# Low parts of transposed probabilities: one VectorE instruction over two PSUM banks in place of one for each bank

## The chip, the cores and the metric

The kernel runs on one core of one Trainium2 chip. The metric is the device time of one execution in microseconds; the median of three runs is given. A profile of one further execution shows each engine's instructions.

## The reference

A batch of 8 images of 128 channels and 32 x 32 positions (N = 1024) goes through two attention layers. All is float32.

```python
# layer 0
theta, phi, g = conv1x1(x, ...), conv1x1(x, ...), conv1x1(x, ...)   # each (B, 128, N)
attn = softmax(einsum('bcn,bcm->bnm', theta, phi), axis=-1)         # (B, N, N)
y = einsum('bnm,bcm->bnc', attn, g).reshape(B, 128, H, W)
z = (1 - w) * x + w * conv1x1(y, wz_w, wz_b)
# layer 1, on z
q, k, v = Wq @ z + bq, Wk @ z + bk, Wv @ z + bv                     # 16, 16 and 128 channels
att = softmax(einsum('bdi,bdj->bij', q, k) / sqrt(16), axis=-1)
out = gamma * einsum('bcj,bij->bci', v, att)
fused = Wf @ concat([out, z]) + bf
```

## The kernel before, in words

To keep float32's precision with the faster fp32r matmuls, an operand is split into a high part (rounded to fp32r) and a low part (the rest, full minus high), and a product is the sum of three matmuls: high x high, high x low, low x high.

**Units and blocks.** A unit is 128 query rows against all 1024 keys. Four units make a block: one layer, one image, one half of the queries. `BLOCKS` lists the 32 blocks, so there are 128 units. The blocks of the two layers alternate. Each engine runs the same hand-written order of steps: `emit(k)` for steps 0 to 19, a loop of 5 trips with 16 steps each, and the steps that are left. The engines meet only through semaphores.

**What happens to unit k.** TensorE makes its scores (two PSUM banks, `unit_scores`). VectorE takes the negated row maximum over both banks (`unit_max`, L751). ScalarE makes the exponentials into `probs` (`unit_exp`, L631). TensorE transposes `probs` in eight 128 x 128 pieces into `trans`, four for each of two PSUM banks (`unit_transposes`, L495). ScalarE copies each bank, rounded, to `pt_hi` (`unit_hi`, L640, two instructions). VectorE makes `pt_lo` = `trans` minus `pt_hi` (`unit_lo`, L761, two instructions, one for each bank). When a block's four units are through, `value_chunk` multiplies `pt_hi` and `pt_lo` by the values' two parts, in four chunks over the next steps (L519 to L521), into the PSUM bank `accum`.

**The order in a step.** On TensorE: scores of k; the small groups that the schedule puts before; the value chunks of the step; the small groups that it puts after; the transposes of k - 1. On ScalarE: the drain of `accum` where one is due; high parts of k - 2; exponentials of k - 1; the small groups. On VectorE: the drain of `accum` where one is due (L828, `o_sb`); a reciprocal once per block; the low parts of k - 2; the small groups before; the maximum of k; the small groups after. So on VectorE all that follows in a step is queued behind the low parts.

**What waits for the low parts.** The transposes of unit k overwrite `trans`, so before its bank 0 and again before its bank 1 TensorE waits for `pt_lo_ready` of unit k - 1 and that bank:

```python
for bank in range(2):
    if k >= 1:
        pe.wait_ge(pt_lo_ready, banks(k - 1, bank, it))
```

`value_chunk` waits for bank 1 of a block's last unit. The last block of all is different: its chunks are cut by bank and by pair of units, each waits for its own bank (`banks(TPB * gb + 2 * pair + 1, part, it)`), and nothing follows them but the last output.

**The small groups** are the projections and the like (theta, phi, g, y, z, qk, v, f, r). All use one PSUM bank, `misc`, one after the other, and TensorE begins one only when the one before has been drained (`misc_drained`). VectorE drains g (L788, L793), v (L793), y (L799), z (L807) and the second halves of qk (L773, L776), after which it copies a part of the keys (L779). GpSimd splits x, g, v, y and z in two parts; the z and y parts are matmul operands later. `r` turns the reciprocals into rows of `r_rows` by two matmuls (L566, L567), and `o_sb` (L828) is `accum` times `r_rows`; it sets `accum` free for the next block's first matmul.

Of the kernel before, what the change touches and what calls it, by code (L numbers as in the profile page):

```python
# [33 lines left out]
P = 128  # L34
HALF = N // 2
TPB = HALF // P
KT = N // P
CPB = 4
# [144 lines left out]
def build(nc, x, x_tiles, weights_t, columns, qk_bias, g_bias, gates, out):  # L183
    f32, f32r = mybir.dt.float32, mybir.dt.float32r
    ALU, ACT, AX = mybir.AluOpType, mybir.ActivationFunctionType, mybir.AxisListType

    with ExitStack() as ctx:
        def sb(name, shape, dt=f32):
            return ctx.enter_context(nc.sbuf_tensor(name, shape, dt))

        def sem(name):
            return ctx.enter_context(nc.semaphore(name))
# [41 lines left out]
        pt_hi = sb("pt_hi", [P, 2, KT, HALF], f32r)  # L234
        pt_lo = sb("pt_lo", [P, 2, KT, HALF], f32r)
# [44 lines left out]
        trans = ctx.enter_context(nc.psum_tensor("trans", [P, N], f32))  # L280
# [24 lines left out]
        pt_hi_ready = sem("pt_hi_ready")  # L305
        pt_lo_ready = sem("pt_lo_ready")
        pv_done = sem("pv_done")
# [29 lines left out]
        def banks(k, bank, it):  # L337
            return 2 * k + bank + 1 + 2 * PERIOD * it
# [4 lines left out]
        def chunks(gb, c, it):  # L343
            return CPB * gb + c + 1 + PERIOD * it
# [17 lines left out]
        def cols(h):  # L362
            return slice(h * HALF, (h + 1) * HALF)

        def f(ap):
            return ap.bitcast(f32)
# [344 lines left out]
        def _(dve):  # L711
# [41 lines left out]

            def unit_lo(k, it):
                gb, t = divmod(k, TPB)
                for bank in range(2):
                    dve.wait_ge(pt_hi_ready, banks(k, bank, it))
                    if t == 0 and bank == 0 and gb >= 2:
                        dve.wait_ge(pv_done, chunks(gb - 2, CPB - 1, it))
                    at = (slice(None), gb % 2, slice(4 * bank, 4 * bank + 4), slice(t * P, (t + 1) * P))  # L760
                    nc.vector.tensor_tensor(pt_lo[at], trans[:, cols(bank)].rearrange("p (n q) -> p n q", n=4),  # L761
                                            f(pt_hi[at]), ALU.subtract).then_inc(pt_lo_ready, 1)

            def small(group, it):
                kind, b, h = group
# [53 lines left out]
            def emit(k, it):  # L819
# [25 lines left out]
                if 0 <= k - 2 < UNITS:  # L845
                    unit_lo(k - 2, it)
# [155 lines left out]
```

## Time and profile before

| | |
|---|---|
| median of 3 runs | 548.36 us (548.23 to 548.5) |
| the profiled execution, its own time | 549.02 us |
| its span, first to last instruction | 547.2 us |
| TensorE busy | 521.3 us, 95% |
| its weight loads | 436.5 us, 80% |
| VectorE busy | 431.9 us, 79% |
| ScalarE busy | 373.1 us, 68% |
| GpSimd busy | 303.4 us, 55% |
| granted TensorE clock | 1.00 over the whole span |

In the profile PE is TensorE's matmuls, PEld its weight loads, DVE is VectorE, ACT ScalarE, POOL GpSimd. Matmuls overlap their neighbours in the trace, so a matmul's own duration is longer than its step in the stream. Consecutive VectorE or ScalarE instructions overlap a little too. L761 is line 761 of the kernel. Times in the timeline are microseconds from the start of the span; `xN` merges N consecutive alike instructions into one row, whose duration is from the first one's start to the last one's end.

### The profile page before, as it was taken

What the parts mean: (1) busy time and instruction counts of PE and PEld (TensorE: products, weight loads), DVE (VectorE), ACT (ScalarE), POOL (GpSimd) and SP (SyncE); (2) the same over time, 40 slices, a digit from 0 to 9 for tenths busy, and PEclk for the clock granted to TensorE, in tenths of its full rate; (3) what the DMA queues carried; (4) which work ended last, traced back from release to release, by engine and by line L of the source; (5) the groups of instructions that cost most, each with busy time, mean ns of one, the idle gap of its engine ahead of it and who ended that gap; (6) DMA issues with size and microseconds to landing.
All of it is one profiled execution on the core that took longest, in us unless ns stands there. A gap on an engine that the chain in (4) does not pass through costs nothing.

```text
span 547.2 us, 9717 instructions
## 1 busy us (share of the span) xinstructions
PE 521.3 (95%) x2933; PEld 436.5 (80%) x2933; DVE 431.9 (79%) x633; ACT 373.1 (68%) x668; POOL 303.4 (55%) x288
## 2 busy tenths in 40 slices
PE   7898899999999989999899998999999999899996
PEld 5677778887888878888788887888788888687886
DVE  5948687798777887888877888679887787989973
ACT  4765577568785678657777577765878557878773
POOL 1576257684277743875448752579426780274442
PEclk9999999999999999999999999999999999999999
DMA  5000000011000100002000020000200010000011
GB/s 171 26 36 2 0 1 0 2 41 59 0 22 0 62 34 0 19 0 96 0 0 19 0 96 0 0 19 4 91 0 0 19 40 20 0 2 20 1 40 38
DMA packets 5782, 13.41 MB, mean 25 GB/s; under 512 B 1024, under 2 KB 1536, under 8 KB 5760
## 3 DMA queue, kind: packets, MB, share of 16 engines
q1 hardware_dynamic: 5616, 13.00, 7.0%
q8 instruction: 12, 0.20, 0.2%
q10 hardware_dynamic: 144, 0.13, 0.1%
q14 instruction: 10, 0.08, 0.1%
HBM read 8.93 MB, written 4.19 MB: 24 GB/s over the span
## 4 chain that ended last, share of the span: by engine, by line
PE 82%; ACT 7%; DVE 5%; issue 4%; POOL 1%; DMA 1%; ACTq 0%; DVEq 0%
PE trans L495 18%; PE accum L519 10%; PE accum L521 9%; PE accum L520 9%; PE scores L485 5%; PE scores L460 5%; PE scores L462 4%; PE scores L461 4%; PE misc L460 3%; PE misc L546 3%; PE misc L462 3%; PE misc L461 3%; ACT probs L631 3%; ACT pt_hi L640 2%; DVE pt_lo L761 2%
## 5 line engine op out<-in xcount | busy, mean ns | idle before, releaser
L761 DVE TENSOR_TENSOR pt_lo<-trans,pt_hi 128x512 fp32r<-128x512 f32 x256 | 164.6, 685 | 56.3 <-ACT pt_hi L640 54.7
L640 ACT ACTIVATE pt_hi<-trans 128x512 fp32r<-128x512 f32 x256 | 139.7, 596 | 74.0 <-PE trans L495 72.8
L751 DVE TENSOR_REDUCE neg_max<-scores 128x1 f32<-128x1024 f32 x128 | 155.6, 1215 | 1.1 <-PE scores L462 1.1
L495 PE MATMUL trans<-ident,probs 128*128 128x128 f32 x1024 | 135.2, 274 | 13.3 <-DVE pt_lo L761 7.3
L631 ACT ACTIVATE probs<-scores,neg_max 128x1024 f32<-128x1024 f32 x128 | 143.7, 1123 | 4.9 <-DVE neg_max L751 4.5
L495 PEld LDWEIGHTS trans<-ident,probs 128*128 128x128 f32 x1024 | 115.3, 141 | 28.4 <-DVE pt_lo L761 9.9
L519 PE MATMUL accum<-pt_hi,g_hi 128*128 128x512 f32 x136 | 54.3, 400 | 0.0
L521 PE MATMUL accum<-pt_hi,g_lo 128*128 128x512 f32 x136 | 53.5, 394 | 0.0
L520 PE MATMUL accum<-pt_lo,g_hi 128*128 128x512 f32 x136 | 53.3, 392 | 0.0
L460 PE MATMUL scores<-phi_hi,theta_hi 128*128 128x512 f32 x112 | 49.0, 437 | 0.2 <-POOL phi_lo L879 0.2
L866 POOL TENSOR_TENSOR theta_hi<-proj_full,zero 128x512 fp32r<-128x512 f32 x14 | 14.6, 1041 | 57.7 <-ACT proj_full L659 57.7
L462 PE MATMUL scores<-phi_hi,theta_lo 128*128 128x512 f32 x112 | 44.2, 395 | 0.0
L461 PE MATMUL scores<-phi_lo,theta_hi 128*128 128x512 f32 x112 | 43.8, 391 | 0.0
L519 PE MATMUL accum<-pt_hi,v_hi 128*128 128x512 f32 x96 | 38.8, 404 | 0.0
L793 DVE TENSOR_TENSOR values_full<-misc,values_full 128x256 f32<-128x256 f32 x64 | 27.1, 423 | 14.0 <-ACT values_full L653 11.9
L521 PE MATMUL accum<-pt_hi,v_lo 128*128 128x512 f32 x96 | 37.7, 392 | 0.0
L520 PE MATMUL accum<-pt_lo,v_hi 128*128 128x512 f32 x96 | 37.6, 392 | 0.0
L866 POOL TENSOR_TENSOR y_hi<-y_full,zero 128x512 fp32r<-128x512 f32 x16 | 16.7, 1041 | 33.6 <-DVE y_full L799 33.6
L866 POOL TENSOR_TENSOR z_hi<-z_full,zero 128x512 fp32r<-128x512 f32 x16 | 16.7, 1041 | 32.9 <-DVE z_full L807 32.9
L485 PE MATMUL scores<-k_op,q_op 96*128 96x512 f32 x96 | 34.2, 437 | 0.0
L521 PEld LDWEIGHTS accum<-pt_hi,g_lo 128*128 128x128 f32 x136 | 25.5, 188 | 5.8
L519 PEld LDWEIGHTS accum<-pt_hi,g_hi 128*128 128x128 f32 x136 | 25.5, 188 | 5.4
(161 smaller groups left out, 1037.2 us busy)
## 6 DMA issues: line engine op xcount, KB each, us to landing
x_keep<-x_dram SPq DMA_DIRECT2D x8, 512.0 KB, 3.4
out_dram<-o_sb SPq DMA_DIRECT2D x15, 256.0 KB, 2.0
x_raw<-x_tiles_dram SPq DMA_DIRECT2D x7, 512.0 KB, 3.7
x_raw<-x_tiles_dram SPq DMA_DIRECT2D x2, 256.0 KB, 3.8
w_all<-weights_t_dram SPq DMA_DIRECT2D x1, 336.0 KB, 3.7
out_dram<-o_sb SPq DMA_DIRECT2D x2, 128.0 KB, 1.9
w_all<-weights_t_dram ACTq DMA_DIRECT2D x1, 128.0 KB, 3.9
g_bias_rows<-g_bias_dram SPq DMA_DIRECT2D x1, 64.0 KB, 3.4
```

The source lines that it names most:

```text
L460: nc.tensor.matmul(dst, hi_l, hi_r, start=True, stop=False)
L461: nc.tensor.matmul(dst, hi_l, lo_r, start=False, stop=False)
L462: return nc.tensor.matmul(dst, lo_l, hi_r, start=False, stop=True)
L485: last = nc.tensor.matmul(dst, q_of(b)[0:KROWS, q0:q0 + P], k_of(b)[0:KROWS, cols(half)], start=True, stop=True)
L495: last = nc.tensor.transpose(trans[:, n * P:(n + 1) * P], probs[:, k % 2, n * P:(n + 1) * P], ident[:, :])
L519: nc.tensor.matmul(dst, hi[:, tile], p_hi, start=(n == 0), stop=False)
L520: nc.tensor.matmul(dst, hi[:, tile], p_lo, start=False, stop=False)
L521: last = nc.tensor.matmul(dst, lo[:, tile], p_hi, start=False, stop=(n == KT - 1))
L631: nc.scalar.activation(probs[:, k % 2, :], scores[:, k % 2, :], ACT.Exp, bias=neg_max[:, k % 4:k % 4 + 1], accum_out=row_sum[:, slot(gb), ...
L640: nc.scalar.activation(pt_hi[:, gb % 2, 4 * bank:4 * bank + 4, t * P:(t + 1) * P], trans[:, cols(bank)].rearrange("p (n q) -> p n q", n=4) ...
L751: nc.vector.tensor_reduce(neg_max[:, k % 4:k % 4 + 1], scores[:, k % 2, :], AX.X, ALU.max, negate=True).then_inc(max_ready, 1)
L761: nc.vector.tensor_tensor(pt_lo[at], trans[:, cols(bank)].rearrange("p (n q) -> p n q", n=4), f(pt_hi[at]), ALU.subtract).then_inc(pt_lo_r ...
```

## The change

`unit_lo` no longer goes bank by bank. It waits until the high parts of both banks are there, and one instruction of 1024 columns subtracts them from both banks of `trans`. Its semaphore rises by 2, so that all who wait for a bank still count alike. The wait for the value chunks of two blocks earlier, which frees the buffer of `pt_lo`, stands before that one instruction as it stood before the first of two.

```diff
             def unit_lo(k, it):
                 gb, t = divmod(k, TPB)
-                for bank in range(2):
-                    dve.wait_ge(pt_hi_ready, banks(k, bank, it))
-                    if t == 0 and bank == 0 and gb >= 2:
-                        dve.wait_ge(pv_done, chunks(gb - 2, CPB - 1, it))
-                    at = (slice(None), gb % 2, slice(4 * bank, 4 * bank + 4), slice(t * P, (t + 1) * P))
-                    nc.vector.tensor_tensor(pt_lo[at], trans[:, cols(bank)].rearrange("p (n q) -> p n q", n=4),
-                                            f(pt_hi[at]), ALU.subtract).then_inc(pt_lo_ready, 1)
+                dve.wait_ge(pt_hi_ready, banks(k, 1, it))
+                if t == 0 and gb >= 2:
+                    dve.wait_ge(pv_done, chunks(gb - 2, CPB - 1, it))
+                at = (slice(None), gb % 2, slice(None), slice(t * P, (t + 1) * P))
+                nc.vector.tensor_tensor(pt_lo[at], trans[:, :].rearrange("p (n q) -> p n q", n=KT),
+                                        f(pt_hi[at]), ALU.subtract).then_inc(pt_lo_ready, 2)
```

## Rows read from the trace of the kernel before

**Rows 1.** The page: busy time by engine, and the chain's shares by engine.
```profile
PE 521.3 (95%) x2933; PEld 436.5 (80%) x2933; DVE 431.9 (79%) x633; ACT 373.1 (68%) x668; POOL 303.4 (55%) x288
...
PE 82%; ACT 7%; DVE 5%; issue 4%; POOL 1%; DMA 1%; ACTq 0%; DVEq 0%
```

**Rows 2.** The chain in order of time (start, duration, what), one unit's transposes.
```profile
252.56 0.88 PE trans L495 x8
```

**Rows 3.** The page's groups: busy us, mean ns | idle before, releaser.
```profile
L761 DVE TENSOR_TENSOR pt_lo<-trans,pt_hi 128x512 fp32r<-128x512 f32 x256 | 164.6, 685 | 56.3 <-ACT pt_hi L640 54.7
...
L751 DVE TENSOR_REDUCE neg_max<-scores 128x1 f32<-128x1024 f32 x128 | 155.6, 1215 | 1.1 <-PE scores L462 1.1
...
L793 DVE TENSOR_TENSOR values_full<-misc,values_full 128x256 f32<-128x256 f32 x64 | 27.1, 423 | 14.0 <-ACT values_full L653 11.9
```

**Rows 4.** The waits: who <- for whom, us in total, times, longest.
```profile
DVE pt_lo L761 <- ACT pt_hi L640: 54.7, 77, 3.4
...
PEld trans L495 <- DVE pt_lo L761: 9.9, 15, 1.6
...
PE trans L495 <- DVE pt_lo L761: 7.3, 6, 1.4
```

**Rows 5.** Timeline, a plain unit (start, duration, engine, line, what).
```profile
282.91 1.09 ACT L640 ACTIVATE pt_hi<-trans 128x512 fp32r<-128x512 f32 x2 [0.60 <-PE trans L495]
...
283.54 1.29 DVE L761 TENSOR_TENSOR pt_lo<-trans,pt_hi 128x512 fp32r<-128x512 f32 x2 [0.86 <-ACT pt_hi L640]
...
284.75 1.22 DVE L751 TENSOR_REDUCE neg_max<-scores 128x1 f32<-128x1024 f32 x1
...
285.72 1.03 PE L495 MATMUL trans<-ident,probs 128*128 128x128 f32 x8
```

**Rows 6.** Timeline, behind the key copy; one of five such places.
```profile
261.73 2.41 DVE L779 CAST k_op<-k_op 32x512 fp32r<-32x512 f32 x1
...
264.17 1.29 DVE L761 TENSOR_TENSOR pt_lo<-trans,pt_hi 128x512 fp32r<-128x512 f32 x2
264.92 0.42 PEld L495 LDWEIGHTS trans<-ident,probs 128*128 128x128 f32 x4 [1.59 <-DVE pt_lo L761]
...
265.51 0.42 PEld L495 LDWEIGHTS trans<-ident,probs 128*128 128x128 f32 x4 [0.18 <-DVE pt_lo L761]
```

**Rows 7.** Timeline, drains of z and of the accumulator in one loop trip.
```profile
315.10 0.75 DVE L807 SCALAR_TENSOR_TENSOR z_full<-misc,gate,x_keep 128x512 f32<-128x512 f32 x1
315.54 1.09 ACT L640 ACTIVATE pt_hi<-trans 128x512 fp32r<-128x512 f32 x2 [1.24 <-PE trans L495]
...
316.24 0.39 PE L566 MATMUL misc<-diag_hi,ones_r 128*128 128x512 f32 x1
...
318.50 0.68 DVE L828 TENSOR_TENSOR o_sb<-accum,r_rows 128x512 f32<-128x512 f32 x1
...
319.44 0.40 PE L519 MATMUL accum<-pt_hi,g_hi 128*128 128x512 f32 x1
```

**Rows 8.** Timeline near the start: what TensorE waited for.
```profile
21.05 0.38 PE L546 MATMUL misc<-w_parts,x_hi 128*128 128x256 f32 x1 [1.01 <-DVE values_full L793]
...
24.85 1.16 PE L495 MATMUL trans<-ident,probs 128*128 128x128 f32 x8 [0.55 <-DVE pt_lo L761]
```

**Rows 9.** Timeline in the last 85 us, a z drain and the matmul behind it.
```profile
478.54 0.74 DVE L807 SCALAR_TENSOR_TENSOR z_full<-misc,gate,x_keep 128x512 f32<-128x512 f32 x1
...
479.50 0.28 PE L546 MATMUL misc<-wv_parts,z_hi 128*128 128x256 f32 x1
```

**Rows 10.** Timeline, transposes released by the exponential with low parts close behind.
```profile
505.08 1.29 DVE L761 TENSOR_TENSOR pt_lo<-trans,pt_hi 128x512 fp32r<-128x512 f32 x2
...
506.14 0.86 PEld L495 LDWEIGHTS trans<-ident,probs 128*128 128x128 f32 x8 [1.07 <-ACT probs L631]
```

**Rows 11.** Timeline, the last unit and the last block's first matmul.
```profile
539.62 1.29 DVE L761 TENSOR_TENSOR pt_lo<-trans,pt_hi 128x512 fp32r<-128x512 f32 x2 [1.93 <-ACT pt_hi L640]
...
540.37 0.39 PE L519 MATMUL scores<-pt_hi,g_hi 128*128 128x256 f32 x1 [0.98 <-DVE pt_lo L761]
```

## The prediction

> **What bounds the kernel now.** I read the page's shares of busy time and its chain first. TensorE is busy for 95% of the span and holds 82% of the chain that ended last; VectorE is busy for 79% and holds 5% of it [rows 1]. So the end is set by TensorE's instruction stream plus the places where that stream stops. VectorE's length as such sets nothing: it is the question of when single VectorE instructions end. The chain prices TensorE's stream: the eight transposes of a unit take 0.88 us when nothing stops them, 0.11 each [rows 2].
>
> Then the groups: the low-part subtractions are 256 instructions of 685 ns, the row maxima 128 of 1215 ns over 1024 columns, and a subtraction-like TENSOR_TENSOR with 256 columns takes 423 ns [rows 3]. Then the waits: VectorE stood idle 54.7 us for the high parts that ScalarE makes, in 77 pieces; TensorE and its weight load stood idle 7.3 and 9.9 us for the low parts, in 6 and 15 pieces [rows 4]. VectorE has time to spare where it waits for ScalarE; TensorE's stops behind it are short and few.
>
> The timeline shows a plain unit [rows 5]. ScalarE makes the two banks' high parts back to back from 282.91, 1.09 us for both. VectorE starts on bank 0 at 283.54, right after the first of them, and runs bank 1 behind it until 284.83; the two halves of the work are a pipeline over the two engines. Only at 285.72 does TensorE come to the next transposes, which overwrite the banks: 0.89 us of slack. The row maximum is queued behind the low parts on VectorE and starts when they end.
>
> **The change part by part.** One instruction of 1024 columns replaces two of 512. Its own duration is not in the trace. From 256 to 512 columns the time grows by 262 ns, so 1024 columns make 685 + 524 = 1209 ns; the maximum over 1024 columns of the same PSUM banks takes 1215 [rows 3]. I take 1.21 us. The pair takes 1.29 us from first start to last end [rows 5], because the second starts under the tail of the first. Bounds: 1.37 us, twice 685, from above; from below 1.07, which is 1024 columns at the 1.02 ns that each further column costs, with almost no fixed part left (1.05).
>
> Removed: 0.08 us of VectorE per unit, 10 us over 128 units, of a 79% busy engine. Where VectorE waits for ScalarE this is worth nothing. Added: the instruction waits for the second bank's high parts. In the plain unit these end at 284.00; a start 0.03 later, as the first low part shows, gives 284.03 to 285.24, against 284.83 [rows 5]. So bank 1's low part ends 0.42 us later, bank 0's about 1.0 later, and the maximum with everything queued behind it on VectorE starts 0.42 later until VectorE next waits for something else. In the plain unit nothing needs this: the transposes have 0.89 us in hand. That covers most units, as the few stops in [rows 4] say.
>
> The move of the wait on the values two blocks earlier costs nothing: that block ended four units before. The signal rises by two in place of one twice; the counts on TensorE's side are the same, but its wait for bank 0 is now met only with bank 1's. No DMA is moved.
>
> The Trainium skill ("Perfetto Trace Analysis", section Optimizing Scalar/DVE Operations) says that larger operations help where the engine is saturated, and that breaking up instructions may let work complete sooner where Vector is not saturated but causes bubbles on other engines. The trace agrees with the second half as the case here (79% busy, stops of TensorE behind the low parts); by the first half alone the change would gain the 1.3 us of rival 3 below.
>
> Where it is on the path, in order of weight:
>
> (a) Once per trip of the loop, five times, the copy of the keys takes 2.41 us, with GpSimd splitting x at its side. The low parts behind it start at 264.17 and end 265.46; TensorE has been idle for 1.59 us and starts four transposes at 264.92, the other four at 265.51, 0.05 after the second low part [rows 6]. After: one instruction 264.17 to 265.38, the first four at 265.43, the second four after 4 x 0.11 = 0.44 at 265.87. That is 0.36 later. VectorE is saturated here and the 0.08 is gained, but it is outweighed since half of the transposes no longer run under the second low part. 5 x 0.36 = 1.8.
>
> (b) Also once per trip, VectorE drains a misc group and the accumulator just in time. z_full ends 315.85, TensorE needs it at 316.24; with 0.42 more and the 0.05 signal it starts at 316.32, a stop of 0.08. The high parts of the next unit end at 316.63, so again VectorE is 0.42 late; o_sb then ends at 319.18 + 0.42 = 319.60, and the first matmul of the next block moves from 319.44 to 319.65 [rows 7]. Together 0.22 per trip, 1.1 for five, and 0.1 for still smaller margins of 0.02 to 0.05 us elsewhere in the trips.
>
> (c) The start. VectorE is full from the first unit's low parts on (setup work). Its 0.42 reaches the drain for which TensorE waited 1.01 us before 21.05, and the next transposes, which waited for the low parts like the 24.85 ones [rows 8], lose (a)'s 0.36: 0.78 together, which I take as 0.75. One more place like (a) in this stretch has a free 0.36. The y drain near 66 us, queued behind the low parts and read by GpSimd before TensorE can go on, loses 0.23; two small ones 0.15. Sum 1.5.
>
> (d) The last 85 us. The z drain that ends at 479.28 releases a matmul at 479.50: with 0.42 and 0.05 it is 479.75, a stop of 0.25 [rows 9]; three drains of this kind I take at 0.25, 0.2 and 0.05 (the first of them again z, the others o_sb). Five transposes wait for the exponential with the low parts close behind: low parts 505.08 to 506.37, transposes at 506.14. After, 506.29 plus 0.05 is 506.34, 0.2 later for the first four and 0.15 for the last four [rows 10]; 0.7 for five. And the last unit: the last block's value matmuls begin on bank 0 alone at 540.37, 0.06 after the first low part's end at 540.31 [rows 11]. With the high parts' second half 0.49 later and 1.21 us for the whole it is 541.32 plus 0.06: 1.0 us later, and nothing after it hides that. Sum 0.25 + 0.5 + 0.7 + 1.0 = 2.45.
>
> Total 1.8 + 1.2 + 1.5 + 2.45 = 6.95, say 7.0 us. The profiled execution took 549.02 us with a span of 547.2; its own time plus 7.0 is 556.0. The runs' median is 548.36, 0.66 below the profiled one, so I state 555.4.
>
> At 1.07 us instead of 1.21 each of (a) to (d) shrinks by 0.14 where it exists: about 5 x (0.22 + 0.08) at the trips, 0.9 at the start, 1.6 at the end, 4.0 in all. At 1.37 each grows by 0.16, and transposes that have only 0.10 to 0.18 in hand after the change begin to stop too: about 1.3 per trip, 2.0 at the start, 3.5 at the end, 12.0 in all.
>
> **Rivals.**
>
> 1. Only the direct losses stay (transposes and value matmuls that waited for the low parts), and the drains are absorbed, for instance because matmul ends are modelled and TensorE's true need is later than shown. Then 1.8 at the trips, 1.1 at the start, 0.7 + 1.0 at the end: 4.6 us, 553.0. For it: the margins in (b) are of 0.1 to 0.2 us. Against it: the drains stand behind an in-order queue, and TensorE's stream around them has no gap.
>
> 2. The instruction costs as much as the two did (1.37), or its effects feed on each other through ScalarE: 12 us, 560.4. Against it: the 1215 ns maximum over the same banks [rows 3].
>
> 3. It gets faster. The mechanism: fewer instructions, 0.08 us saved in each unit in which VectorE is the bound. At the bound of all 128 units this would be 10 us, but the chain gives VectorE 5% [rows 1], and only about 16 units have low parts that queue behind other VectorE work: 16 x 0.08 = 1.3 us, 547.1. It decides from the point at which TensorE gets nothing from the early release of bank 0. In [rows 6] it does start on it, 0.59 us before the rest, and the last block does as well [rows 11]; I see no place where only VectorE's sum counts. The Trainium skill ("VectorE: DVE Perf Modes", section Rules for kernel authors) advises to minimize the op count; by that rule it would come out this way.
>
> 4. No difference: all 0.42 us delays find slack and (a) is made good by the saved 0.08 and by later gaps. 548.4. Against it stands the last unit's 1.0 us, which no gap follows.
>
> **How the numbers follow.** My forecast 0.57 (its own range 554 to 557.5), rival 1 0.20, rival 2 0.14, rival 3 0.04, no difference 0.05. What a measurement of this kernel can tell from no change is about 0.2%, 1.1 us. Faster 0.04, same 0.05, slower 0.91. The range takes in rival 1 and the 1.07 bound (552.4) below, and goes most of the way to rival 2 above: 551.8 to 559.5.
>
> **What would show it.** 128 low-part instructions of about 1.21 us; VectorE's busy time down, its idle time for the high parts up by well over 20 us. In the five places behind the key copy, transposes that start as one run of eight, with TensorE's idle time before them about 0.5 us longer. New stops of TensorE at the `r` group, at the first matmul of a block behind o_sb, and at v groups behind z_full. The last block's first matmul, 0.75 us after the last pair of low parts began, would come 1.27 us after the one instruction's start. A duration near 1.37, or low parts that start later than 0.05 us after the high parts, would make the prediction too low; TensorE idle for low parts unchanged would make it too high.

## The result and the profile after

The changed kernel takes 565.08 us, median of 4 runs (562.94 to 569.53), against 548.43 (548.23 to 549.88) for the kernel before: ratio 1.0305, 95% interval 1.027 to 1.0339, so 3% slower. The direction was forecast; the time lies outside the stated range of 551.8 to 559.5 and the rise is 16.7 us where 7.0 was forecast. The profiled execution took 562.94 us with a span of 561.1, 13.9 more than the span of before.

The page of the changed kernel, busy time and chain:

```profile
PE 527.9 (94%) x2933; PEld 438.1 (78%) x2933; DVE 420.8 (75%) x505; ACT 372.6 (66%) x668; POOL 303.4 (54%) x288
...
PE 78%; DVE 8%; ACT 6%; issue 5%; POOL 1%; DMA 1%; ACTq 0%; DVEq 0%
```

Against [rows 1] VectorE is busy 11 us less with 128 instructions fewer, and yet its share of the chain rises from 5 to 8%. TensorE is busy 6.6 us more for the same 2933 matmuls. Nobody gave it work: some of its matmuls ran slower. That was the first sign of what the prediction had no term for.

The groups and the waits of the changed kernel, which answer to [rows 3, 4]:

```profile
L760 DVE TENSOR_TENSOR pt_lo<-trans,pt_hi 128x1024 fp32r<-128x1024 f32 x128 | 156.8, 1225 | 100.6 <-ACT pt_hi L640 90.7
```

```profile
DVE pt_lo L760 <- ACT pt_hi L640: 90.7, 97, 3.6
...
PE trans L495 <- DVE pt_lo L760: 19.3, 20, 2.0
...
PEld trans L495 <- DVE pt_lo L760: 13.0, 15, 2.2
```

The merged instruction takes 1225 ns; 1.21 us had been taken for it. What VectorE saved it spent waiting for ScalarE: 36 us more of idle time in front of the low parts. TensorE waits for the low parts 19.3 us in 20 places, where it was 7.3 in 6, and the longest such stop grew from 1.4 to 2.0 us.

A plain unit after the change, for [rows 5]:

```profile
290.99 1.09 ACT L640 ACTIVATE pt_hi<-trans 128x512 fp32r<-128x512 f32 x2 [0.60 <-PE trans L495]
292.18 1.23 DVE L760 TENSOR_TENSOR pt_lo<-trans,pt_hi 128x1024 fp32r<-128x1024 f32 x1 [0.93 <-ACT pt_hi L640]
293.32 1.21 DVE L751 TENSOR_REDUCE neg_max<-scores 128x1 f32<-128x1024 f32 x1
293.80 1.03 PE L495 MATMUL trans<-ident,probs 128*128 128x128 f32 x8
```

The high parts end at 292.08 and the low parts start at 292.18, 0.10 later; the trace of before had led me to expect 0.03. From the first high part's start to the low parts' end it is 2.42 us, where it was 1.92: VectorE's queue is 0.50 us late in each such unit, not 0.42. The transposes still come in time here, with 0.39 us in hand.

Behind the key copy, for [rows 6], once at TensorE's full clock and once, one trip earlier, as it also happened:

```profile
201.19 2.36 DVE L778 CAST k_op<-k_op 32x512 fp32r<-32x512 f32 x1
...
203.57 1.23 DVE L760 TENSOR_TENSOR pt_lo<-trans,pt_hi 128x1024 fp32r<-128x1024 f32 x1
204.85 1.57 PEld L495 LDWEIGHTS trans<-ident,probs 128*128 128x128 f32 x8 [2.20 <-DVE pt_lo L760]
204.85 1.97 PE L495 MATMUL trans<-ident,probs 128*128 128x128 f32 x8 [2.05 <-DVE pt_lo L760]
...
206.47 0.78 PE L460 MATMUL scores<-phi_hi,theta_hi 128*128 128x512 f32 x1
...
271.86 1.23 DVE L760 TENSOR_TENSOR pt_lo<-trans,pt_hi 128x1024 fp32r<-128x1024 f32 x1
273.13 0.86 PEld L495 LDWEIGHTS trans<-ident,probs 128*128 128x128 f32 x8 [2.14 <-DVE pt_lo L760]
```

In both places the eight transposes now start as one run after the low parts' end. In this document a stop is the idle time of TensorE's matmuls, here the 2.05 us in the row of PE at 204.85; its weight load stood idle 2.20. At 273.13 their weight loads take 0.86 us, at 204.85 they take 1.57, and the next scores matmul 0.78. The windows of the changed kernel around the earlier place (columns as in their first line) say why:

```profile
core 0: us, PE busy (x) PEld busy (x) DVE busy (x) ACT busy (x) POOL busy (x), PEclk, DMA share, GB/s
200.00:204.00 4.00, 2.81 (x15) 2.25 (x13) 3.90 (x4) 3.58 (x7) 3.19 (x2) 1.00 0.00 0
204.00:208.00 4.00, 3.15 (x12) 2.86 (x13) 2.79 (x5) 2.17 (x4) 1.34 (x3) 0.59 0.00 0
208.00:212.00 4.00, 4.00 (x23) 3.41 (x22) 2.31 (x3) 1.55 (x4) 1.11 (x2) 0.98 0.00 0
```

After a stop of 2.05 us TensorE's granted clock is 0.59 in the next 4 us, that is the lower level of 1.2 GHz most of the time, and the unit and its successor together come 1.6 us later than the same two do at the other four trips. Before the change the same stops were of 1.2 to 1.4 us and the granted clock stayed at 1.00.

The drains, for [rows 7]:

```profile
323.89 0.74 DVE L806 SCALAR_TENSOR_TENSOR z_full<-misc,gate,x_keep 128x512 f32<-128x512 f32 x1
324.75 0.19 PEld L566 LDWEIGHTS misc<-diag_hi,ones_r 128*128 128x128 f32 x1 [0.48 <-issue]
324.76 0.49 PE L566 MATMUL misc<-diag_hi,ones_r 128*128 128x512 f32 x1
...
327.30 0.68 DVE L827 TENSOR_TENSOR o_sb<-accum,r_rows 128x512 f32<-128x512 f32 x1
...
328.03 0.19 PEld L519 LDWEIGHTS accum<-pt_hi,g_hi 128*128 128x128 f32 x1 [0.26 <-DVE o_sb L827]
```

Both stops that (b) named are there. Their price was set too low: the drain's signal reaches the weight load 0.12 us after z_full's end (0.05 after o_sb's), and the weight load now starts only behind the stop. The matmul takes 0.49 us where it took 0.39 [rows 7], and the next one follows it after 0.33 us instead of 0.23. The g drain ahead of z's matmuls had shown the longer way of the signal before the change: it ends at 301.47 and the weight load follows 0.13 later.

```profile
301.05 0.42 DVE L793 TENSOR_TENSOR values_full<-misc,values_full 128x256 f32<-128x256 f32 x1
...
301.60 0.19 PEld L460 LDWEIGHTS misc<-y_hi,w_parts 128*128 128x128 f32 x1
```

Close behind the exponential, for [rows 10], and the last unit, for [rows 11]:

```profile
516.90 1.22 DVE L760 TENSOR_TENSOR pt_lo<-trans,pt_hi 128x1024 fp32r<-128x1024 f32 x1
518.24 0.86 PEld L495 LDWEIGHTS trans<-ident,probs 128*128 128x128 f32 x8 [1.35 <-ACT probs L631]
518.27 0.95 PE L495 MATMUL trans<-ident,probs 128*128 128x128 f32 x7 [0.95 <-DVE pt_lo L760]
...
553.01 1.22 DVE L760 TENSOR_TENSOR pt_lo<-trans,pt_hi 128x1024 fp32r<-128x1024 f32 x1 [2.38 <-ACT pt_hi L640]
554.28 0.19 PEld L519 LDWEIGHTS scores<-pt_hi,g_hi 128*128 128x128 f32 x1 [2.30 <-DVE pt_lo L760]
```

Near 518 the low parts end at 518.12 and the transposes follow 0.12 later: they, and no longer the exponential alone, release them. At the last unit the first matmul comes 1.27 us after the low parts' start, as forecast.

Laying the two traces over each other, unit by unit at the last of its eight transposes, gives where the 13.9 us of the profiled execution came from. Worked out from the starts of those transposes:

```
stretch                                   after - before   forecast
ahead of the first low part                    1.7            -
start, up to the first loop trip               1.5           1.5
five loop trips, without the next line         5.1           3.0
lower clock after the stop at 204.85           1.6            -
behind the loop, with the last unit's 1.1      3.9           2.45
```

The first 1.7 us lie ahead of the first low part, where both programs are the same. TensorE's matmuls follow each other there at 0.43 us in place of 0.23 for some microseconds longer. First the kernel before, then the changed one:

```profile
7.60 0.40 PE L460 MATMUL scores<-x_hi,w_parts 128*128 128x512 f32 x1
...
7.83 0.40 PE L461 MATMUL scores<-x_lo,w_parts 128*128 128x512 f32 x1
```

```profile
7.36 0.63 PE L460 MATMUL scores<-x_hi,w_parts 128*128 128x512 f32 x1
...
7.79 0.63 PE L461 MATMUL scores<-x_lo,w_parts 128*128 128x512 f32 x1
```

0.63 us and a step of 0.43 are also what such a matmul takes at the lower clock behind the stop at 204.85 (207.05, 207.47), so this too is TensorE at its lower level. The profile prints 1.00 there because the traces hold no record of the clock before 5.05 us (before) and 10.17 us (after), and the steps are of 0.43 us ahead of these places and of 0.23 behind them; "1.00 over the whole span" in the table of before is to be read so. This long start is no effect of the change. Of the fourteen traces of this case ten start so, with the first transposes at 16.0 to 16.5 us, and in six of these nothing is merged; the other four have them at 14.3 to 14.5, and one of the four is merged from the first unit on. Nor is the kernel before free of the clock's fall later on: 12 of the 56 executions of it that were run beside the experiments have a granted clock of 0.997, as the profiled one of the changed kernel has with its one fall. Of these 12 there is no trace.

### The profile page after: what moved, and what is told of

The parts are those of the page before. It is cut to its first block, busy times and chain, and to the rows that moved or that the text cites. A ratio compares the mean times of both kernels' runs of the same rounds, so it can differ in the third digit from the quotient of the medians.

```text
span 561.1 us, 9612 instructions
## 1 busy us (share of the span) xinstructions
PE 527.9 (94%) x2933; PEld 438.1 (78%) x2933; DVE 420.8 (75%) x505; ACT 372.6 (66%) x668; POOL 303.4 (54%) x288
## 2 busy tenths in 40 slices
DMA packets 5782, 13.41 MB, mean 24 GB/s; under 512 B 1024, under 2 KB 1536, under 8 KB 5760
## 4 chain that ended last, share of the span: by engine, by line
PE 78%; DVE 8%; ACT 6%; issue 5%; POOL 1%; DMA 1%; ACTq 0%; DVEq 0%
PE trans L495 17%; PE accum L519 9%; PE accum L521 9%; PE accum L520 9%; PE scores L460 5%; PE scores L462 4%; PE scores L461 4%; PE scores L485 4%; DVE pt_lo L760 4%; PE misc L460 3%; PE misc L546 3%; PE misc L462 3%; PE misc L461 3%; ACT pt_hi L640 3%; PE misc L547 1%
## 5 line engine op out<-in xcount | busy, mean ns | idle before, releaser
L760 DVE TENSOR_TENSOR pt_lo<-trans,pt_hi 128x1024 fp32r<-128x1024 f32 x128 | 156.8, 1225 | 100.6 <-ACT pt_hi L640 90.7
L495 PE MATMUL trans<-ident,probs 128*128 128x128 f32 x1024 | 135.0, 275 | 19.3 <-DVE pt_lo L760 19.3
L865 POOL TENSOR_TENSOR z_hi<-z_full,zero 128x512 fp32r<-128x512 f32 x16 | 16.7, 1041 | 37.6 <-DVE z_full L806 37.5
L865 POOL TENSOR_TENSOR y_hi<-y_full,zero 128x512 fp32r<-128x512 f32 x16 | 16.7, 1043 | 34.8 <-DVE y_full L798 34.8
L865 POOL TENSOR_TENSOR g_hi<-values_full,zero 128x512 fp32r<-128x512 f32 x18 | 18.8, 1044 | 20.9 <-DVE values_full L792 20.9
```

Of the source, the lines that this page charges most:

```text
L495: last = nc.tensor.transpose(trans[:, n * P:(n + 1) * P], probs[:, k % 2, n * P:(n + 1) * P], ident[:, :])
L760: nc.vector.tensor_tensor(pt_lo[at], trans[:, :].rearrange("p (n q) -> p n q", n=KT), f(pt_hi[at]), ALU.subtract).then_inc(pt_lo_ready, 2)
L865: return nc.gpsimd.tensor_tensor(hi, full, zero[:, :].broadcast_to([P, full.shape[1]]), ALU.add)
```

## The experiments

Each ratio is to runs of the kernel before on the same chip, given with its median.

**Both halves wait for both high parts.** Two instructions stay, but start when the merged one would.

```diff
-                    dve.wait_ge(pt_hi_ready, banks(k, bank, it))
+                    dve.wait_ge(pt_hi_ready, banks(k, 1, it))
```

> Two low-part instructions as before the change, but both wait for the high parts of both banks. Theory (timing): the loss comes from when VectorE starts and from TensorE being released late, not from the merged instruction. Then this kernel, whose second low part ends even some 0.07 us later than the merged one, must be slower than before by 6 to 8 us (555 to 557), with the stops behind the key copy unchanged at about 1.4 us (there the high parts are long ready) and a granted clock of 1.00. Rival (size): one instruction over two PSUM banks is itself what costs. Then this is within 1 us of before, 548.4.

555.69 us against 549.60, ratio 1.0098 (1.0065 to 1.0131), granted clock 1.00 in three executions and 0.997 in two, where 1.00 had been expected. The longest stop of TensorE for low parts is 1.5 us. Nothing is merged here and most of the direct loss in the loop's drains is there: the same transposes as in the changed kernel come 0.20, 0.30 and 0.1 us late in each trip, those behind the key copy are within 0.16 us of where they were. The rival (the large instruction as such) falls.

**Both halves at their times, TensorE told only at the end.**

```diff
-                                            f(pt_hi[at]), ALU.subtract).then_inc(pt_lo_ready, 1)
+                                            f(pt_hi[at]), ALU.subtract)
+                    if bank == 1:
+                        last.then_inc(pt_lo_ready, 2)
```

> Two low-part instructions at their old times, but TensorE is told of both only when the second has ended. Theory (timing): this isolates the loss of bank 0's early release. VectorE's queue is untouched. Key copy: 5 x 0.4 = 2.0 us; three such places in the first 80 us 1.1; five transposes close behind the exponential 0.7; last block 0.6. Sum 4.4, so 552.8; the stop behind the key copy becomes 2.0 us, and if such a stop is what lowers TensorE's clock, 0 to 5 us more and a granted clock below 1.00 in some executions. Rival (size): 548.4, no change.

557.22 us, ratio 1.0128 (1.0088 to 1.0168), granted clock 0.990 to 0.993 in all four executions. The trace against that of before: 0.5 us at two units near the start, 0.3 to 0.45 behind the key copy, 0.34 at three of the five units close behind the exponential, nothing at the drains; about 4 us in all up to the last unit. Another 3.1 us lie at the low clock after two stops of 1.93 us, of which this is the first:

```profile
267.57 1.29 DVE L761 TENSOR_TENSOR pt_lo<-trans,pt_hi 128x512 fp32r<-128x512 f32 x2
268.92 1.25 PEld L495 LDWEIGHTS trans<-ident,probs 128*128 128x128 f32 x7 [2.08 <-DVE pt_lo L761]
```

The two parts add up, nearly: without start and clock the trace of both_wait is 5.1 us late at the last unit's transposes and that of late_signal 4.0; the changed kernel's is 9.5.

**The changed kernel with two halves behind the key copy.** `unit_lo` takes the old form for k == 26, which in the loop is that unit of each trip.

> The changed kernel, but with two instructions in the one unit per loop trip whose low parts stand behind the key copy. Theory (timing and clock): the stop there stays at about 1.4 us, each trip gives back 0.4 to 0.5, and TensorE's clock stays at 1.00: 557 to 559, with runs close together. Rival (clock by chance): the clock still falls to 0.98 to 0.99 in some executions and the runs spread over several us as those of the changed kernel did (562.9 to 569.5).

560.08 us, ratio 1.0196 (1.0152 to 1.024), 5.0 us below the changed kernel's median. That is above the 557 to 559 expected. In the trace the stops there are again 1.2 to 1.4 us and the clock does not fall behind them; the runs spread over 2.4 us where the changed kernel's spread over 6.6. The clock was not at 1.00, though (0.996 to 0.997 in all four): in the trace it fell once behind another stop, of 1.83 us near 474 us, at which the exponential of ScalarE is late as well. The kernel before has that stop too, of 1.80 us, and its trace passed it at full clock.

**A longer stop and nothing merged.**

```diff
+                if k == 26:
+                    nc.vector.tensor_tensor(scratch[:, :], w_all[:, 0:HALF], w_all[:, 256:256 + HALF], ALU.add)
                 for bank in range(2):
```

> The kernel before, nothing merged, with one more VectorE instruction (a sum of two pieces of the weights into a scratch tile that nobody reads, about 0.7 us) ahead of the low parts behind the key copy, once per loop trip. TensorE's stop there grows from 1.4 to about 2.1 us: 5 x 0.65 = 3.2 us, 551.7 by length alone. Theory (clock by length of the stop): the granted clock falls below 1.00 in some executions and the runs spread, up to 5 us more. Rival (clock by chance, or only by the merged instruction): 551.7 and 1.00 in all.

560.40 us, ratio 1.0179 (1.0136 to 1.0221), granted clock 0.985 to 0.988 in all four. In the trace four of the five lengthened stops (1.91 to 2.11 us; the fifth is 1.84) are followed by the lower clock, and so is the stop of 1.82 us near 480 us, at about 1.6 us each. The second one:

```profile
202.54 0.69 DVE L758 TENSOR_TENSOR scratch<-w_all 128x512 f32<-128x512 f32 x1
203.24 1.29 DVE L764 TENSOR_TENSOR pt_lo<-trans,pt_hi 128x512 fp32r<-128x512 f32 x2
203.99 0.42 PEld L496 LDWEIGHTS trans<-ident,probs 128*128 128x128 f32 x4 [2.26 <-DVE pt_lo L764]
```

Its windows have the granted clock at 1.00, then 0.59:

```profile
200.00:204.00 4.00, 1.89 (x12) 1.48 (x10) 3.92 (x5) 3.08 (x5) 2.23 (x1) 1.00 0.00 0
204.00:208.00 4.00, 4.00 (x15) 3.24 (x16) 3.25 (x6) 2.29 (x4) 1.61 (x4) 0.59 0.00 0
```

So 0.7 us of VectorE work in five places costs about 10 us (by the ratio 9.8, 7.5 to 12.1), where some 8 at most had been expected: in the trace five lowered clocks came on top of the longer stops. The clock falls because TensorE stood still for long, not because of the merged instruction.

**The merged instruction in the unit behind the key copy alone.** k == 26 only.

> The kernel before, with the merged instruction only in the unit behind the key copy, five units in all. Theory (gate and clock): about 0.45 us directly in each, 2.2 us, and stops of 1.9 us that lower the clock in several of them at 1.0 to 1.6 us each: 551 to 556, clock 0.99. Theory without the clock: 550.6 and 1.00.

556.13 us, ratio 1.0119 (1.0077 to 1.016), granted clock 0.987 to 0.997, three lowered clocks in the trace, behind stops of 1.90, 1.90 and 1.81 us. The time is at the upper end of what was expected, 551 to 556. Five instructions of 128 carry a good third of the change's whole loss.

**The merged instruction where it is covered.** 28 <= k < 33, 25 units.

> The kernel before, with the merged instruction only in five units per loop trip (25 of 128) at whose transposes the changed kernel's trace shows no shift. Theory (a VectorE that waits gives nothing back): within 0.2% of before, clock 1.00. Rival (each merged unit saves or costs by itself): 2 us less (25 x 0.08) or about 2.7 us more (25/128 of the whole loss).

549.02 us against 550.18, ratio 0.9998 (0.9978 to 1.0018). In the trace the last unit's transposes are 0.03 us from where they were. The 2 us that VectorE saves are worth nothing, and a delay of 0.5 us costs nothing either where TensorE comes later anyway.

**The merged instruction in the last unit alone.** k == 127.

> The kernel before, with the merged instruction only in the last of the 128 units, in front of the last block's value matmuls, which start on bank 0's low part. Theory: the last block's first matmul 1.0 to 1.1 us later and the end with it, as nothing follows that could hide it: 549.5 on runs of 548.4, the stop there 2.1 us in place of 1.0. Rival (the end is set by r_rows or the store): no change.

Ratio 1.0023 (1.0008 to 1.0037), that is 1.3 us with an interval of 0.4 to 2.0; TensorE's stop ahead of the last block is 2.07 us.

**The changed kernel again.**

> The changed kernel once more, on the same chip as the run beside it, to see the spread of its clock. Theory: the direct loss of some 10.6 us is in every execution, on top come 0 to 2 us at the start as in the kernel before, and 1 to 1.6 us for each stop of about 2 us after which the clock is lowered, one to five of them: 561 to 569, with the granted clock between 0.98 and 1.00 and the longer times at the lower clocks. Rival (the spread is not the clock): times and granted clocks unrelated.

564.82 us, ratio 1.0295 (1.0239 to 1.0351). Over the eight executions of the changed kernel, time and granted clock go together:

```
us      562.82  562.94  562.98  564.04  566.12  566.67  569.53  569.84
clock   0.997   0.997   0.994   0.990   0.990   0.990   0.981   0.984
```

The profiled one has three lowered clocks inside the loop, behind stops of 1.92, 2.03 and 2.10 us, and stands 3.7 us behind the other at the last unit.

**Taking the stop away.** The key copy is slow only beside GpSimd's split of x. First the split was moved two steps later.

```diff
-SPLIT_X = {3: 1, 14: 2, **{LOOP_FROM + PERIOD * (i - 2) + 9: i + 1 for i in range(2, B - 1)}}
+SPLIT_X = {3: 1, 14: 2, **{LOOP_FROM + PERIOD * (i - 2) + 11: i + 1 for i in range(2, B - 1)}}
```

> The kernel before, nothing merged, with GpSimd's split of the next x two steps later in the loop, after its work on the reciprocals, so that it no longer runs beside VectorE's key copy. The copy should take about 0.42 us in place of 2.4, the low parts behind it start some 2 us earlier, and TensorE's stop of 1.4 us per trip go. The next projections need the split only some 2 us after its new end. Theory (the key copy's stop is the place where a low part decides): 5 x 1.1 to 1.4 = 5.5 to 7 us less than before, 541.5 to 543. Rival (GpSimd or ScalarE is late next): 546 to 549.

546.93 us against 550.18, ratio 0.9944 (0.9928 to 0.9959). The first copy now takes 0.42 us and 1.7 us come back in each trip, but the second key copy of the trip has become the slow one:

```profile
270.82 2.40 POOL L873 TENSOR_TENSOR x_lo<-x_raw,x_hi 128x1024 fp32r<-128x1024 f32 x1
...
271.31 2.18 DVE L779 CAST k_op<-k_op 32x512 fp32r<-32x512 f32 x1
...
274.27 0.42 PEld L495 LDWEIGHTS trans<-ident,probs 128*128 128x128 f32 x4 [1.19 <-DVE pt_lo L761]
```

It gives 1.05 back, so that neither my estimate nor its rival held: the collision moved. The Trainium skill ("SBUF — State Buffer", section SBUF: two separate sides) says that VectorE and GpSimd share a port pair that one of them holds alone; by the 0.42 us without and 2.0 to 2.4 us with a neighbour, the traces agree, and the slow copy above ends 0.27 us after GpSimd's instruction does (273.49 and 273.22).

The same later split under the changed kernel:

> The changed kernel (merged instruction) with the same later split of x. Theory: the direct loss and the lowered clock behind the key copy go with the stop, the losses at the drains stay: 541.5 to 543 plus some 8 to 9 us (0.6 per trip, 1.5 at the start, 3.9 at the end), so 550 to 552, the clock lowered at most once near 468 us (a stop of 2.0 us there). Rival (the merged instruction spoils the clock wherever it stands): 556 or more and a clock of 0.99.

558.37 us, ratio 1.0169 (1.0137 to 1.0202), granted clock 0.997 to 1.000. By the medians that is 11.4 us above late_split, but the median of late_split lies between two groups of its executions (545.65 to 546.33 and 547.54 to 548.17). Both traces have the long start, and their spans of 556.6 and 546.4 are 10.3 us apart: the direct loss by itself, at the full clock. I had expected 550 to 552. The later split gave less than I thought, and behind the two key copies the merged instruction still loses some 0.4 us per trip.

Then the split was held until the first copy is done, and so lies between the two.

```diff
                 pool.wait_ge(x_loaded, 16 * b + 16 * it)
+                if b >= 3:
+                    pool.wait_ge(k_copied, halves(b - 2, 0, it))
```

In guarded_split the wait stood ahead of the loop too (b == 2, for both copies); guarded_loop has it as shown.

> The kernel before, nothing merged; GpSimd's split of the next x keeps its place but waits for the key copy beside which it ran (k_copied), so that it lies between the two key copies of a trip. The later split only moved the collision to the second copy (2.18 us there, TensorE 1.05 us later per trip). Theory: both copies take 0.42 us, no such stop is left: 1.6 us less per trip than before, 8 us, and about 0.5 us less in the first 80 us: 540 to 542, clock 1.00. Rival (the reciprocals' split on GpSimd, now 1 to 2 us later, is late for the r group): 543 to 547.

> As guarded_split, but with the wait for the key copy only in the loop. Ahead of the loop the wait had put the split 4 us later and the next step 1.8 us back, against 0.3 gained. Theory: another 1.5 us less, 541.5 to 542.5. Rival (the lost 1.8 us is made good later anyway): 543.4.

guarded_split: 543.39 us, ratio 0.9886 (0.9867 to 0.9906), where 540 to 542 had been expected; 1.8 us were lost ahead of the loop. guarded_loop: 542.33 us against 550.04, ratio 0.9857 (0.9834 to 0.988), granted clock 1.00 in all five. Its trace at a key copy:

```profile
260.20 0.42 DVE L779 CAST k_op<-k_op 32x512 fp32r<-32x512 f32 x1
...
260.65 1.29 DVE L761 TENSOR_TENSOR pt_lo<-trans,pt_hi 128x512 fp32r<-128x512 f32 x2
260.70 1.89 POOL L866 TENSOR_TENSOR x_hi<-x_raw,zero 128x1024 fp32r<-128x1024 f32 x1 [7.32 <-DVE k_op L779]
261.77 0.86 PEld L495 LDWEIGHTS trans<-ident,probs 128*128 128x128 f32 x8
```

The low parts start right behind a short copy and TensorE has no stop. This version, with the two halves kept, beats both kernels.

## Why the prediction was wrong

**Right: what bounds the kernel, and the sign.** TensorE's stream and its stops set the end. VectorE's saved time is worth nothing (quiet_only), the second half's high part and bank 0's lost early release cost (both_wait, late_signal). Rival 3, by which fewer instructions gain, is refuted. Rival 1, that the drains are absorbed, is too: both_wait loses at the drains. Rival 2 has a total of 12 us, near the direct loss, but not by its cause: the instruction takes 1.225 us and not 1.37, and both_wait and late_signal add up to nearly the whole, which leaves little for effects that feed on each other. Rival 4, no difference, is outside the interval.

**Right in size: (a), the start and the last unit.** Behind the key copy 0.28 to 0.53 us a trip, 0.39 in the mean, against 0.36, with the lowered clock left out; 1.5 us at the start as forecast; 1.1 us at the last unit against 1.0.

**Failed, first: the sum had no term for TensorE's clock.** The step is (a)'s "That is 0.36 later". It let a stop of 1.4 us grow to some 1.9 and priced only the growth. The traces show that stops of 1.8 to 2.1 us are often followed by the lower clock, at about 1.6 us each, and that shorter ones, in any of the fourteen traces, never were. That longer_stop has the same fall with nothing merged shows the cause. How often it happens differs from execution to execution (one fall and three in the two traces of the changed kernel, after five stops of 1.89 to 2.10 us in the loop each), which goes with the runs' spread from 562.8 to 569.8. No rival had this mechanism; the line on what would make the prediction wrong did not name it either. The trace of before did not show it: its granted clock is 1.00 from 5.05 us to the end, also behind its longest stop, 1.80 us near 468 us.

**Failed, second: (b), mis-sized.** The drains in the loop were put at 1.2 us; they cost about 0.6 per trip, 3.1 in all: about 0.3 at the r group, 0.1 at the first matmul behind o_sb and 0.2 at z's matmuls. The terms: VectorE's queue is 0.50 us late and not 0.42 (low parts start 0.10 and not 0.03 after the high parts; 1.225 us and not 1.21); the signal to a weight load takes 0.12 and not 0.05 in several of these places; a restarted matmul delays the next one by another 0.1 us. The g drain that releases z's matmuls shows it: put at a margin of 0.02 to 0.05 us and 0.02 of cost, it cost 0.20 in each trip. The prediction had named low parts that start more than 0.05 us after the high parts as a sign that it was too low, and that sign came.

**Failed, third: (d), mis-sized by the same terms.** 3.9 us against 2.45. The five units close behind the exponential were put at 0.15 each; four of them lost 0.28 to 0.29. The drain at 479.5 was put at 0.25 and lost 0.44, one near 498 lost 0.45.

The direct loss in the trace is 10.6 us, 559 on a median of 548.4, which is just inside the range. late_split_merged shows 10.3 at the full clock. What goes beyond it is the clock: 1.6 us in the first profiled execution and, by the granted clocks (three falls give 0.990 in the second trace), an estimated 4.8 us in the two executions between which the median of 565.08 lies. The rest is the long start, which came with both kernels.

**Open.** Why a stop of 1.8 to 2.1 us lowers the clock in one trip and not in the next, with the same work before it, was not settled, nor which stops of the kernel before do it in its executions at 0.997. Why low parts start 0.10 us after the second high part but 0.03 after the first was not tried.

## What to carry to other kernels

Merging two instructions of an engine that waits for a neighbour takes apart the pipeline between the two: the merged one starts when the last of its inputs is there and releases nothing before its end, and the fixed part that it saves falls into idle time. Before such an edit, list every place in which the engine behind it waits, add the restart of that engine to the delay, and look at how long its longest stops become: one that was harmless at 1.4 us often cost 1.6 us more at 1.8 to 2.1. The same list shows where to gain: here one stop of 1.4 us per trip came from two engines colliding over a copy, and taking it away gave 1.4%.

## What the runs showed of the hardware

- TensorE's granted clock fell to 1.2 GHz after single stops of 1.81 to 2.11 us, though not after each of them, between stretches in which it was busy without a break, and back within the next 4 to 8 us (0.59, then 0.98 in windows of 4 us). I had not expected this of stops so short. No shorter stop in the fourteen traces was followed by it.
- A VectorE copy of 32 x 512 takes 0.42 us alone and 2.0 to 2.4 us beside a GpSimd TENSOR_TENSOR of 1024 columns.
- VectorE's one instruction over two PSUM banks takes 1225 ns, less than the 1.29 us of two in a row, so reading across a bank's end costs nothing that can be seen.
- At the start TensorE's lower level lasted until 4.3 to 5.6 us of the span in four traces and until 9.7 to 10.9 in ten, which moves the first low parts by about 1.7 us under the same program.
